# Cross-attention split on GpSimd: one subtraction for both rests, one instruction for each side's two middle parts

## The chip, the cores and the metric

The kernel runs on one core of a Trainium2 chip. The metric is the device time of one launch in microseconds (us). Engines are named as in the profile: PE is TensorE, PEld its weight loads, DVE VectorE, ACT ScalarE, POOL GpSimd, SP SyncE.

## What is computed

One decoder layer in float32 over 32 batch items of 128 rows and 128 channels, in three parts, each followed by a layer norm of the sum with its input: a self-attention with quantised weights, a cross-attention with 16 heads of 8 channels, and a mixture of 8 experts of which each row takes two. The change lies in the cross-attention:

```python
qh = proj(q, Wq, bq); kh = proj(k, Wk, bk); vh = proj(v, Wv, bv)      # 16 heads of 8
scores = jnp.einsum('bhqd,bhkd->bhqk', qh, kh) / jnp.sqrt(hd)
w = jax.nn.softmax(jnp.where(m, -jnp.inf, scores), axis=-1)
out = jnp.einsum('bhqk,bhkd->bhqd', w, vh)
```

## The kernel before, in words

The queries and keys are float32, the matmuls of the scores run in bfloat16. So each value is written as a sum of three bfloat16 parts, high, middle and low, and the parts are laid out in six slots of eight columns for every head (tile `QK`, which the profile calls pair_sq since it shares that memory), so that one matmul over the 48 columns gives the sum of the six products that matter. Queries hold high in slots 0, 2, 4, middle in 1 and 3, low in 5; keys hold high in 3, 4, 5, middle in 0 and 1, low in 2. Behind the slots lie pad columns: the mask, and three parts of minus the row maximum.

The cross-attention is staged by an order written out by hand. A slot handles several batch items at different stages, each engine runs its part of the slot (`b_slot`) in program order, and semaphores join them. Four slots make a tile of four items; the slots are numbered j = 1, 2, 3, 0. Per item, in the order of the work:

- PE projects; DVE adds the biases (line 2190 values, line 2191 `qk_f`, queries and keys together).
- ACT writes the high parts into all their slots (lines 1546 and 1547).
- POOL makes the rest and the other parts (lines 844 to 861). First two subtractions, line 845, one for each side: rest = value minus high. Then a wait for them (`ch.settle()`), the mask column (line 849), four copies of the rest into the middle slots that round it to bfloat16 (line 853), a wait, and two subtractions rest minus middle for the low slots (line 857). The last signals `split_ready`.
- In the next slot PE turns the keys (second half of the 16 transposes of line 1107), waiting for `split_ready`; then the queries.

In the same slot DVE works for other items: the maxima of the scores of an earlier item (line 2179, two halves), the row sums of another (2196 to 2200), a copy of turned keys out of PSUM (2207), and then the chain that splits minus the row maximum into three bfloat16 parts (lines 2215, 2217, 2219, 2221, 2223; five instructions on 16 columns, each waiting for the one before). I call these five the maximum chain. After it a slot's own extra follows: j = 1 picks experts (lines 2025 to 2041), j = 2 the sum and statistics of the second norm (2011, 1861, 1872, 1876), j = 3 places rows (2017, 2047 to 2065).

On POOL, ahead of the split, stand the indirect DMAs that post rows for the experts (line 825, two in a slot), in j = 3 the power of line 802, and in j = 0 the copy and numbering of rows (815, 816). `qk_rest` is only used on POOL.

Of the kernel before, what the change touches and what calls it, by code (L numbers as in the profile page):

```python
# [8 lines left out]
def decoder_layer(nc, x, ctx_1024, mask, wq, wk, wv, wo, Wq, bq, Wk, bk, Wv, bv,  # L9
# [3 lines left out]
    ALU, ACT, AX = mybir.AluOpType, mybir.ActivationFunctionType, mybir.AxisListType  # L13

    B, P, D = x.shape
    H, HD = 16, D // 16
# [31 lines left out]
    with ctx:  # L48
        def sb(name, shape, dt=F32):
            return ctx.enter_context(nc.sbuf_tensor(name, shape, dt))  # L50
# [8 lines left out]
        def after(eng, s, n):  # L59

            eng.wait_ge(s, n + CREDIT)
# [5 lines left out]
        class Chain:  # L67
# [129 lines left out]
        QK = pair_sq[:].rearrange("p a b -> p (a b)").bitcast(BF16)[:, 0:8 * H * HS].rearrange(  # L197
            "p (a b c d) -> p a b c d", a=4, b=2, c=H)
# [64 lines left out]
        qk_f = sb("qk_f", [P, 2, 2, D])  # L263
        qk_rest = sb("qk_rest", [P, 2, D])
# [181 lines left out]
        def batch(t, i):  # L446

            return bass.ds(TB * t + i, 1)
# [35 lines left out]
        def slots(j, side, first, end, by=1):  # L484

            return QK[:, j, side, :, 0:6 * HD].rearrange("p h (s d) -> p h s d", d=HD)[:, :, first:end:by, :]

        def heads(ap):

            return ap.rearrange("p (h d) -> p h d", h=H)  # L490
# [28 lines left out]
        def route_turn(u):  # L519

            return 0 <= u - 3 < T - 1
# [127 lines left out]
        def _(pool):  # L649
            ch = Chain(pool, pool_chain)  # L650
# [148 lines left out]
            def invert_roots(u):  # L799

                after(pool, ve2_ready, u - 1)
                pool.tensor_tensor(rstd2[:], ve2[:], half[:, 0:TB], ALU.pow).then_inc(rstd2_ready, 1)

            def preset_rows():

                after(pool, y_rounded, T)
                ch(pool.memset(staged_h[:, :, :, :, D - 1], X_SCALE))
                pool.memset(staged_h[:, :, :, :, 2 * D - 1], 0.0).then_inc(rows_preset, 1)

            def number_rows(t):  # L810

                if t >= 2:
                    posted_by(pool, t - 2)
                pool.wait_ge(x_lo_ready, t + 1)
                ch(pool.tensor_copy(staged_h[:, t % 2, :, 1, D:2 * D - 1], staged_h[:, t % 2, :, 0, D:2 * D - 1]))
                ch(pool.iota(staged[:, t % 2, :, :, D].bitcast(I32), pattern=[[P, TB], [B * P, 2]], base=NT * t,
                             channel_multiplier=1))
                ch.settle()
                pool.wait_ge(spot_ready, t + 1)
                if t == 0:  # L820
                    pool.wait_ge(padded, 16 * PADS)

            def post_rows(t, i, a):

                pool.indirect_dma_start(xs[:], bass.IndirectOffsetOnAxis(ap=spot_u[:, t % 2, a, i:i + 1], axis=0),  # L825
                                        staged[:, t % 2, i, a, :], None).then_inc(posted[t % 2], 16)

            def b_slot(u, parity, there, j):
                if u == 2 and j == 0:
                    preset_rows()  # L830
                if route_turn(u - 1):
                    if j == 0:
                        number_rows(u - 4)
                    for a in range(2):
                        post_rows(u - 4, j, a)
                k = TB * u + j - 1
                if j == 3 and there(2) and not (isinstance(u, int) and u == T + 1):
                    invert_roots(u)
                l, i = divmod(j - 1, TB)
                if there(-l):  # L840

                    after(pool, split_ready, k)
                    after(pool, high_ready, k + 1)
                    for side in range(2):
                        ch(pool.tensor_tensor(heads(qk_rest[:, side]), heads(qk_f[:, i % 2, side]),  # L845
                                              slots(i, side, 4, 5)[:, :, 0, :], ALU.subtract))
                    ch.settle()

                    pool.tensor_tensor(QK[:, i, 1, :, 6 * HD], ones[:, 0:H],
                                       mask_neg[:, batch(u + l, i)].broadcast_to((P, H)), ALU.mult)  # L850
                    for side, (first, end, by) in enumerate(((1, 4, 2), (0, 2, 1))):
                        for s in range(first, end, by):
                            ch(pool.tensor_scalar(slots(i, side, s, s + 1)[:, :, 0, :],  # L853
                                                  heads(qk_rest[:, side]), 1.0, None, ALU.mult))
                    ch.settle()
                    for side, low in enumerate((5, 2)):
                        last = pool.tensor_tensor(slots(i, side, low, low + 1)[:, :, 0, :], heads(qk_rest[:, side]),
                                                  slots(i, side, 1, 2)[:, :, 0, :], ALU.subtract)
                        if side == 0:
                            ch(last)  # L860
                    last.then_inc(split_ready, 1)
# [4 lines left out]
            prepare_pads()  # L866
            y_rows(T - 2)
            one_slot(b_slot, 0, 1)
            first_scales(T - 2)
            one_slot(b_slot, 0, 2)  # L870
            y_stats(T - 1)
            y_rows(T - 1)
            one_slot(b_slot, 0, 3)
            prepare_frames()
            one_slot(b_slot, 1, 0)
# [1585 lines left out]
```

## Time and profile before

| what | value |
|---|---|
| device time, median of 3 runs | 703.71 us (701.25 to 704.7) |
| device time of the profiled execution | 700.64 us |
| span of the profiled execution | 698.9 us |
| DVE busy | 554.2 us (79%) |
| PE busy | 536.1 us (77%) |
| POOL busy | 476.9 us (68%) |
| ACT busy | 475.1 us (68%) |

The span runs from the first to the last instruction; the rest of the profiled execution's time, 1.74 us, lies around it. The self-attention takes the first 215 us or so, the split of the cross-attention runs from 225 to 480 us, and the experts and the last norm follow. Busy shares are means over these stages, so they do not say which engine sets the pace in one of them; the chain of waits and the timeline of a stretch do.

### The profile page before, as it was taken

What the parts mean: (1) busy time and instruction counts of PE and PEld (TensorE: products, weight loads), DVE (VectorE), ACT (ScalarE), POOL (GpSimd) and SP (SyncE); (2) the same over time, 40 slices, a digit from 0 to 9 for tenths busy, and PEclk for the clock granted to TensorE, in tenths of its full rate; (3) what the DMA queues carried; (4) which work ended last, traced back from release to release, by engine and by line L of the source; (5) the groups of instructions that cost most, each with busy time, mean ns of one, the idle gap of its engine ahead of it and who ended that gap; (6) DMA issues with size and microseconds to landing.
All of it is one profiled execution on the core that took longest, in us unless ns stands there. A gap on an engine that the chain in (4) does not pass through costs nothing.

```text
span 698.9 us, 19343 instructions
## 1 busy us (share of the span) xinstructions
PE 536.1 (77%) x6294; PEld 439.6 (63%) x6308; DVE 554.2 (79%) x1699; ACT 475.1 (68%) x975; POOL 476.9 (68%) x655
## 2 busy tenths in 40 slices
PE   1588889998989856878787878877679999997200
PEld 0277878777879845656565656655458889886200
DVE  4999899999996577687979889798778756687584
ACT  4666689887984565778877887777645555667415
POOL 6367688877886274655678898787557776577653
PEclk9789999999999957899999999999699999999655
DMA  6711222222122524354410100001132333531241
GB/s 173 235 13 20 24 22 25 23 23 25 22 39 64 174 86 151 137 220 152 191 49 23 38 32 30 19 19 36 52 92 83 100 102 102 162 111 48 78 118 60
DMA packets 113106, 55.39 MB, mean 79 GB/s; under 512 B 70624, under 2 KB 103840, under 8 KB 113024
## 3 DMA queue, kind: packets, MB, share of 16 engines
q1 hardware_dynamic: 103984, 25.46, 16.2%
q10 hardware_dynamic: 4496, 19.02, 6.9%
q0 software_dynamic: 4544, 9.84, 4.0%
q8 instruction: 49, 0.80, 0.5%
q14 instruction: 33, 0.27, 0.1%
HBM read 21.25 MB, written 33.05 MB: 78 GB/s over the span
## 4 chain that ended last, share of the span: by engine, by line
PE 34%; DVE 32%; ACT 14%; issue 10%; DMA 4%; POOL 3%; SPq 1%; ACTq 0%; DVEq 0%; POOLq 0%
PE PS L996 11%; DVE m L2179 5%; DVE PS L1916 3%; ACT W_raw L1559 3%; PE PS L1289 2%; PE PS L1306 2%; DVE bn L1861 2%; PE PS L1308 2%; PE PS L1307 2%; DMA W_raw<-in_L_ffn_W_dram 2%; PE PS L1107 2%; DVE W_raw L2292 2%; PE PS L1291 1%; PE PS L1290 1%; PE PS L1117 1%
## 5 line engine op out<-in xcount | busy, mean ns | idle before, releaser
L996 PE MATMUL PS<-prod,ident 128*128 128x144 f32 x1024 | 137.4, 294 | 8.5 <-DVE hctx L1896 8.2
L996 PEld LDWEIGHTS PS<-prod,ident 128*128 128x128 f32 x1024 | 131.6, 196 | 16.3 <-issue 9.1
L765 POOL TENSOR_TENSOR prod<-prod,v 128x2048 f32<-128x2048 f32 x32 | 117.5, 3672 | 31.2 <-ACT prod L1403 31.2
L885 POOL DMA_INDIRECT ys<-W_raw,ids x78 | 76.5, 981 | 29.7 <-issue 18.9
L2179 DVE TENSOR_REDUCE m<-PS 128x8 f32<-128x1024 f32 x64 | 77.8, 1216 | 21.1 <-PE PS L1117 21.1
L2292 DVE SCALAR_TENSOR_TENSOR W_raw<-PS,W_raw 128x512 f16<-128x512 f32 x78 | 52.1, 688 | 36.1 <-ACT W_raw L1624 36.1
L825 POOL DMA_INDIRECT xs<-Y,spot_u x64 | 64.2, 1003 | 23.3 <-issue 13.5
L1916 DVE TENSOR_REDUCE PS<-pair_sq 128x128 f32<-128x1024 f32 x64 | 75.0, 1219 | 0.0
L1117 PE MATMUL PS<-prod 52*128 52x128 bf16 (+1 forms) x1024 | 52.6, 230 | 29.2 <-ACT W_raw L1559 11.6
L1559 ACT ACTIVATE W_raw<-PS 128x1024 f32<-128x1024 f32 x64 | 66.0, 1032 | 5.7 <-PE PS L1117 5.7
L853 POOL TENSOR_SCALAR pair_sq<-qk_rest 128x128 bf16<-128x128 f32 x128 | 68.1, 553 | 0.0
L1107 PE MATMUL PS<-ident,pair_sq 128*128 128x128 bf16 x768 | 59.1, 232 | 9.0 <-ACT prod L1552 8.9
L1107 PEld LDWEIGHTS PS<-ident,pair_sq 128*128 128x128 bf16 x768 | 50.7, 104 | 18.1 <-ACT prod L1552 13.8
L1117 PEld LDWEIGHTS PS<-prod 52*128 52x128 bf16 (+1 forms) x1024 | 31.1, 99 | 48.9 <-ACT W_raw L1559 15.6
L1308 PE MATMUL PS<-W_lo,W_raw 128*128 x312 | 59.7, 221 | 0.0
L1307 PE MATMUL PS<-W_hi,W_raw 128*128 x312 | 59.5, 221 | 0.0
L1306 PE MATMUL PS<-W_hi,W_raw 128*128 x312 | 59.4, 221 | 0.0
L845 POOL TENSOR_TENSOR qk_rest<-qk_f,pair_sq 128x128 f32<-128x128 f32 x64 | 25.9, 426 | 45.5 <-ACT pair_sq L1547 45.2
L1546 ACT CAST pair_sq<-qk_f 128x384 bf16<-128x384 f32 x32 | 16.4, 511 | 54.7 <-DVE qk_f L2191 53.3
L1624 ACT ACTIVATE W_raw<-PS 128x512 f16<-128x512 f32 x78 | 45.4, 595 | 10.3 <-PE PS L1291 8.0
L1640 ACT ACTIVATE W_raw<-PS,w_rows 128x128 f32<-128x128 f32 x78 | 24.3, 364 | 39.1 <-PE PS L1308 36.9
L1200 PE MATMUL PS<-W_raw 128*32 128x128 f32 x1024 | 43.8, 292 | 6.6 <-issue 4.8
(321 smaller groups left out, 1535.9 us busy)
## 6 DMA issues: line engine op xcount, KB each, us to landing
xs<-pad ACTq DMA_DIRECT2D x16, 1152.0 KB, 4.7
Y<-xs SPq DMA_DIRECT2D x39, 144.0 KB
W_raw<-ys SPq DMA_DIRECT2D x16, 256.0 KB, 3.2
W_raw<-in_L_ffn_W_dram SPq DMA_DIRECT2D x1, 2048.0 KB
shuffle<-hctx SPq DMA_DIRECT2D x32, 64.0 KB, 3.0
Y<-shuffle SPq DMA_DIRECT2D x32, 64.0 KB, 1.8
cs<-in_ctx_dram SPq DMA_DIRECT2D x8, 256.0 KB
out_dram<-W_raw SPq DMA_DIRECT2D x8, 256.0 KB, 2.3
```

The costliest lines, as they stand in the source:

```text
L765: pool.tensor_tensor(rows[:, :, 0:D].rearrange("p t (d h) -> p t d h", d=HD), a.broadcast_to((P, H, HD, H)), v.broadcast_to((P, H, HD, H)) ...
L853: ch(pool.tensor_scalar(slots(i, side, s, s + 1)[:, :, 0, :], heads(qk_rest[:, side]), 1.0, None, ALU.mult))
L885: pool.indirect_dma_start(ys[:], bass.IndirectOffsetOnAxis(ap=ids[:, j % KD, s:s + 1].bitcast(U32), axis=0), ou[j % OD][:, s, :], None).th ...
L996: last = pe.matmul(PS[:, 6, 0:TC], ident[:], prod2[:, i % 2, TC * t:TC * (t + 1)], start=(t == 0), stop=(t == H - 1))
L1107: last = pe.transpose(PS[:, bank, g * 64:(g + 1) * 64].bitcast(BF16), QK[:, j, side, HR * g:HR * g + HR, :].rearrange("p h r -> p (h r)"), ...
L1117: last = pe.matmul(PS[:, 2 * a + r, g * P:(g + 1) * P], left[rows, HG // 2 * a + g, :], right[rows, HG // 2 * a + g, :], start=True, stop= ...
L1306: pe.matmul(o, h_hi[j % 2][:, c, tokens], w_hi, start=False, stop=False)
L1307: pe.matmul(o, h_lo[j % 2][:, c, tokens], w_hi, start=False, stop=False)
L1308: last = pe.matmul(o, h_hi[j % 2][:, c, tokens], w_lo, start=False, stop=(c == FC - 1))
L1559: act.activation(half_heads(PT[:, i % 2], a), banks(a).rearrange("p r (g q) -> p r g q", q=P), ACT.Exp, scale=HD ** -0.5).then_inc(p_ready, 1)
L1916: step(dve.tensor_reduce(total, pair_sq[:, i % 2, HD * first_sum:HD * end_sum].rearrange("p (c d) -> p c d", d=HD), AX.X, ALU.add))
L2179: dve.tensor_reduce(half_heads(m2[:], a), banks(a).rearrange("p r (g t) -> p r g t", t=P), AX.X, ALU.max).then_inc(max_done, 1)
```

## The change

The two subtractions of line 845 become one, over both sides (256 elements in each partition instead of 128). The wait between them and the mask column goes. The four copies of line 853 become two subtractions, one for each side: value minus high, written into both middle slots at once (256 elements, both inputs read twice through a broadcast), rounded to bfloat16 on the way out. They read `qk_f` and the high slot, no longer the rest. The wait before the low parts and the two instructions of line 857 stay.

```diff
-                    for side in range(2):
-                        ch(pool.tensor_tensor(heads(qk_rest[:, side]), heads(qk_f[:, i % 2, side]),
-                                              slots(i, side, 4, 5)[:, :, 0, :], ALU.subtract))
-                    ch.settle()
+                    both = QK[:, i].rearrange("p a h r -> p (a h) r")
+                    ch(pool.tensor_tensor(qk_rest[:].rearrange("p a (h d) -> p (a h) d", h=H),
+                                          qk_f[:, i % 2].rearrange("p a (h d) -> p (a h) d", h=H),
+                                          both[:, :, 4 * HD:5 * HD], ALU.subtract))
 
                     pool.tensor_tensor(QK[:, i, 1, :, 6 * HD], ones[:, 0:H],
                                        mask_neg[:, batch(u + l, i)].broadcast_to((P, H)), ALU.mult)
                     for side, (first, end, by) in enumerate(((1, 4, 2), (0, 2, 1))):
-                        for s in range(first, end, by):
-                            ch(pool.tensor_scalar(slots(i, side, s, s + 1)[:, :, 0, :],
-                                                  heads(qk_rest[:, side]), 1.0, None, ALU.mult))
+                        ch(pool.tensor_tensor(slots(i, side, first, end, by),
+                                              heads(qk_f[:, i % 2, side]).unsqueeze(2).broadcast_to((P, H, 2, HD)),
+                                              slots(i, side, 4, 5).broadcast_to((P, H, 2, HD)), ALU.subtract))
                     ch.settle()
```

## Rows read from the trace of the kernel before

**Rows 1.** Chain of waits: start us, length us, engine, tile, line.

```profile
308.64 0.23 DVE pair_sq L2217
...
399.93 0.09 DVE m_neg L2215
...
400.55 0.23 DVE pair_sq L2221
...
400.93 0.69 DVE yq_f L2011
...
469.27 0.24 DVE pair_sq L2217
```

**Rows 2.** DVE's waits from 330 to 476 us: us, times, longest us.

```profile
DVE m L2179 <- PE PS L1117: 8.8, 4, 3.2
```

**Rows 3.** Timeline of DVE in a j = 0 slot: start, us, line, operation, shape.

```profile
417.44 1.23 DVE L2179 TENSOR_REDUCE m<-PS 128x8 f32<-128x1024 f32 x1 [1.67 <-PE PS L1117]
```

**Rows 4.** Timeline of the j = 2 slot that the working follows.

```profile
397.09 0.42 DVE L2191 TENSOR_TENSOR qk_f<-PS,b_qkv 128x256 f32<-128x256 f32 x1
...
398.62 0.81 POOL L845 TENSOR_TENSOR qk_rest<-qk_f,pair_sq 128x128 f32<-128x128 f32 x2 [0.92 <-ACT pair_sq L1547]
...
399.50 0.27 POOL L849 TENSOR_TENSOR pair_sq<-ones,mask_neg 128x16 bf16<-128x16 f32 x1
...
399.68 2.31 POOL L853 TENSOR_SCALAR pair_sq<-qk_rest 128x128 bf16<-128x128 f32 x4
...
402.08 0.81 POOL L857 TENSOR_TENSOR pair_sq<-qk_rest,pair_sq 128x128 bf16<-128x128 f32 x2
...
403.49 1.06 PE L1107 MATMUL PS<-ident,pair_sq 128*128 128x128 bf16 x16
```

**Rows 5.** POOL's groups by shape: count, busy us, mean ns of one, idle before.

```profile
L765 POOL TENSOR_TENSOR prod<-prod,v 128x2048 f32<-128x2048 f32 x32 | 117.5, 3672 | 31.2 <-ACT prod L1403 31.2
...
L853 POOL TENSOR_SCALAR pair_sq<-qk_rest 128x128 bf16<-128x128 f32 x128 | 68.1, 553 | 0.0
...
L845 POOL TENSOR_TENSOR qk_rest<-qk_f,pair_sq 128x128 f32<-128x128 f32 x64 | 25.9, 426 | 45.5 <-ACT pair_sq L1547 45.2
...
L896 POOL TENSOR_TENSOR X<-X,bet 128x512 f32<-128x512 f32 x8 | 10.1, 1261 | 0.0
```

**Rows 6.** Timeline of two stretches where small DVE instructions meet POOL's.

```profile
414.08 0.82 POOL L845 TENSOR_TENSOR qk_rest<-qk_f,pair_sq 128x128 f32<-128x128 f32 x2
...
414.59 0.37 DVE L2217 CAST pair_sq<-m_neg 128x16 bf16<-128x16 f32 x1
...
471.35 0.48 DVE L2056 TENSOR_SCALAR Y<-w_first,o_scale 128x4 f32<-128x4 f32 x1
471.38 0.81 POOL L857 TENSOR_TENSOR pair_sq<-qk_rest,pair_sq 128x128 bf16<-128x128 f32 x2
...
471.75 0.47 DVE L2057 SCALAR_TENSOR_TENSOR Y<-w_first,o_scale,eg 128x4 f32<-128x4 f32 x1
...
472.13 0.61 POOL L815 COPY Y<-Y 128x508 f16<-128x508 f16 x1
472.26 0.50 DVE L2061 TENSOR_TENSOR run<-run,picked 128x8 bf16<-128x8 bf16 x1
```

**Rows 7.** Single lines of DVE: count, duration in ns min/median/max, first and last start.

```profile
L2217 DVE CAST pair_sq<-m_neg x32: 203/223/380, 254.6 to 490.2; 128x16 bf16<-128x16 f32 x32
...
L2221 DVE CAST pair_sq<-m_rest x32: 205/224/244, 255.2 to 490.7; 128x16 bf16<-128x16 f32 x32
...
L2035 DVE CAST topf<-topi x8: 181/318/431, 333.5 to 531.7; 128x32 f32<-128x32 uint32 x8
...
L2056 DVE TENSOR_SCALAR Y<-w_first,o_scale x8: 231/280/481, 347.9 to 535.3; 128x4 f32<-128x4 f32 x8
...
L2057 DVE SCALAR_TENSOR_TENSOR Y<-w_first,o_scale,eg x8: 212/220/468, 348.3 to 535.4; 128x4 f32<-128x4 f32 x8
...
L2061 DVE TENSOR_TENSOR run<-run,picked x8: 154/160/500, 348.8 to 535.7; 128x8 bf16<-128x8 bf16 x8
```

## Prediction, made before the result was known

> **What bounds the kernel now.** I read the profile's busy shares first (the table above), then the chain of waits, then the timeline of single slots. The shares say little here: DVE, PE, POOL and ACT are all between 68 and 79% busy over the whole span. The chain says more. From about 300 to 476 us it runs through DVE in most slots, one instruction behind the other, the maximum chain among them. Its cast of line 2217 stands on the chain 15 times between 308.64 and 469.27 us [rows 1]. These are the batch items 9, 12 to 14, 16 to 18, 20 to 22, 24, 25 and 28 to 30, counted from 0. In the other slots DVE waits for PE: after 330 us four times ahead of line 2179, 8.8 us together, all in j = 0 slots [rows 2], 1.67 us in the one that I show [rows 3].
>
> POOL's split is on no path. In the j = 2 slot shown, the last low part is done at 402.08 + 0.81 = 402.89 us, and PE begins its 16 transposes, of which the second half reads the keys, at 403.49 [rows 4]. So a faster split is waited for by nobody. What it can do is meet other work.
>
> **What the change does to POOL.** I count from the end of `qk_f`, 397.09 + 0.42 = 397.51 us. Before: rests from +1.11, mask at +1.99, four copies from +2.17 to +4.48, low parts from +4.57 to +5.38 [rows 4]. Price of the new instruction, a tensor_tensor on 256 elements, which the trace does not show: 128 elements take 0.426 us, 2,048 take 3.672 [rows 5], a slope of 1.69 ns, so 0.64 us. With 512 elements at 1.261 us [rows 5] as the other end the slope is 2.17 ns and the price 0.70. The cheap end comes from the mask, 16 elements in 0.27 us [rows 4]: a slope of 1.39 ns from there to 128, so 0.60. I take 0.64, since line 765, the only one of them with a broadcast of three levels, lies on that line. Neighbours overlap by 0.04 us (two of 0.426 take 0.81 [rows 4, 5]), and from mask to the next instruction it is 0.18 [rows 4].
>
> After: rest +1.11 to +1.75; mask at +1.71; first middle pair +1.89 to +2.53; second +2.49 to +3.13; the wait that stays, 0.08; low parts +3.21 to +4.02. POOL saves about 1.1 us for each of 32 items, some 35 us of busy time, and the wait that went (0.08) is in it. The posts of the next slot (line 825) start so much earlier when their addresses are there; on the chain nobody waits for them in this stage. Worth of all this on the path: zero, and its cover is the 0.6 us between 402.89 and 403.49, which only grows.
>
> **What it does to DVE.** The maximum chain starts at 399.93, +2.42, and the next instruction (line 2011) at 400.93, +3.42 [rows 1]. Before, all of it lay beside the four copies of line 853. After, it lies beside the second middle pair and the low parts, which are tensor_tensor. That is not the same to DVE, as the trace shows.
>
> Beside tensor_tensor: at 414.59 the cast of line 2217 takes 0.37 us in place of 0.20, and ends 0.06 behind the second L845 (414.08 + 0.82 = 414.90) [rows 6, 7]. At 471.35 line 2056 takes 0.48 in place of 0.23, at 471.75 line 2057 takes 0.47 in place of 0.21, each ending just behind one of the two L857 that run back to back from 471.38 to 472.19; and line 2061 takes 0.50 in place of 0.15, ending behind the copy of line 815 at 472.74 [rows 6, 7]. So a small DVE instruction on SBUF that meets one of these on POOL waits until it ends, and the two alternate: each POOL instruction costs one DVE instruction its length.
>
> Beside the copies of line 853 nothing of this happens: line 2221, at 400.55 in the midst of them [rows 1, 4], never takes over 0.244 us in 32 executions, against 0.205 at best; the median loss is 0.02 [rows 7].
>
> The Trainium skill (SBUF — State Buffer, section "Who interferes with whom") says that VectorE and GpSimd share a pair of ports, that whichever instruction issues first holds it to its end, and that the order of issue decides and not the kind of operation. The tensor_tensor rows agree with it; line 853, a tensor_scalar that reads SBUF as well, does not. By the rule the copies would have held DVE up just as long, and less POOL time could only help; that is the third rival below.
>
> So the chain after: line 2215 starts at +2.42 and waits for the first middle pair until about +2.56, 0.05 later than before. Line 2217 waits for the second pair, +3.13, and ends near +3.19. Line 2219 then starts behind the first low part (+3.21) and waits for its end, +3.64; line 2221 waits for the second, +4.02, and ends near +4.07; line 2223 starts at +4.10 and the next instruction 0.12 behind it, +4.22. Before it was +3.42. **The price is 0.8 us for an item whose maximum chain is on the path.** If line 2219 slips in front of the first low part, one wait falls away and it is some 0.3 less. The second pair ends at 1.21 + 3 times the price of an instruction: at 0.70 us an item costs 1.0, at 0.60 it costs 0.7, and 0.4 if line 2219 slips in as well.
>
> What comes back: line 2035 met the low parts in the j = 1 slots (median 0.318 against 0.181 [rows 7]), and POOL will be done by then: 0.14 an item, with line 2038 about 0.2. Lines 2056, 2057 and 2061 lost 0.25, 0.26 and 0.35 in two j = 3 slots, at item 30 [rows 6] and alike at item 14, near 348 us (their first starts in [rows 7]); that is 0.85 for each, less about 0.1 for the copy of line 815, which then runs earlier and meets them.
>
> **The sum.** j = 2, the 6 items 9, 13, 17, 21, 25, 29: 6 x 0.8 = 4.8. j = 1, the 5 items 12, 16, 20, 24, 28: 5 x (0.8 - 0.2) = 3.0. j = 3, items 18 and 22: 2 x 0.8 = 1.6; items 14 and 30: 0.8 - 0.75, nothing. Together 9.4 us. All other items have slack: in the j = 0 slots the 1.67 us [rows 3] takes up 0.8, and item 26, which is not on the chain, ends in the longest of the four waits, 3.2 us [rows 2]. Against the profiled execution: 700.64 (span 698.9 and 1.74 around it) + 9.4 = 710.0. That execution is 3.1 us, 0.4%, under the median of the three runs; from the median, 703.71, the same sum gives **713.1**, and I name 713.
>
> Ends: all items at 0.4 give 2.4 + 1.0 + 0.8 less 0.7 for items 14 and 30, 3.5, or 707.2. All at 1.0 give 6.0 + 4.0 + 2.0 + 0.5, with item 26 coming onto the path 1.0 more, 13.5, or 717.2. From the profiled execution the low end is 704.1.
>
> **The rivals.** First, the new subtractions are dearer: 256 elements as two of 128, 0.81 us. Then the second pair ends at 1.21 + 3 x 0.81 = +3.64, the next instruction starts at +4.73, and an item costs 1.3: 6 x 1.3 + 5 x 1.1 + 2 x 1.3 + 2 x 0.55 + 1.3 = 18.3, or 722. Against it: from 128 to 512 elements the time grows 3.0 times, to 2,048 only 8.6 times [rows 5].
>
> Second, the small DVE instructions are not held by the new forms: both their inputs read bfloat16 and float32 through broadcasts, and no row shows that form beside them. Then only what comes back is left, 5 x 0.2 + 2 x 0.75 = 2.5: 701.2, within the bound. For it: of the forms that hold DVE, lines 845, 857 and 815, none has three levels. Against it: their length and kind, two inputs, are the same.
>
> Third, on the other side: **DVE gets there first and POOL is the one that waits.** In the slot shown the four copies take 2.31 us in place of four at about 0.5, since line 2011 runs beside them [rows 4]; so POOL does wait for DVE. If every POOL instruction that reads SBUF holds DVE alike or not at all, as line 853 does, then what stands beside DVE falls from 4.27 us (+1.11 to +5.38) to 2.91 an item, and DVE gets back all that it lost: 5 x 0.2 + 2 x 0.85 = 2.7 us, and the 0.02 that three of the five instructions lose on each of the 15 items, 0.9. Together 3.6 us, 700.1, just beyond the bound. The rule of the Trainium skill named above (SBUF — State Buffer) leads here. It decides from the point where a maximum chain passes three tensor_tensor instructions without a wait. Against it are the rows of lines 2056, 2057 and 2061.
>
> **How the numbers follow.** My forecast, 0.4 to 1.0 us for an item, 72%. The dearer instruction 8%. Not held 15%. POOL waits 5%. The forecast and the first rival are slower by over 0.5%, about what a measurement of this kernel tells from no change (3.5 us, so above 707.2); the second rival is within 0.5%, the third is faster. So faster 0.05, same 0.15, slower 0.80. The range runs from 705, about the low end against the profiled execution, to 719, the high end of the forecast and some of the dearer instruction.
>
> **What would show it.** In the changed profile: POOL's new tensor_tensor on 256 elements at 0.60 to 0.70 us; its split done at about +4.0 behind `qk_f`; lines 2217 and 2221 with medians near 0.4 us where they have 0.22 now, line 2219 likewise; the period of the j = 1 and j = 2 slots longer by 0.6 and 0.8 us; the median of line 2035 at 0.18; nobody waiting for the low parts, as now. It is wrong if those medians stay at 0.2, or if the j = 0 slots show no wait any more, which would mean that their slack was too small for 0.8 us.

## The result, and the profile after

The changed kernel takes 714.77 us, the median of 4 runs (712.93 to 716.0), beside 702.48 us (699.95 to 704.7) for the kernel before: ratio 1.017, 95% interval 1.0137 to 1.0202, so 12.3 us slower. 713 was predicted. The profiled execution of the changed kernel has a span of 714.3 us.

POOL is less busy and DVE more. Page of the changed kernel, busy time (before, in the table above: DVE 554.2, POOL 476.9 us):

```profile
PE 541.4 (76%) x6308; PEld 443.9 (62%) x6308; DVE 576.8 (81%) x1699; ACT 475.7 (67%) x975; POOL 442.5 (62%) x559
```

POOL saves 34.4 us, and DVE is 22.6 us longer busy with the same instructions. The groups of POOL by shape, changed kernel, which answer to [rows 5] (busy us, mean ns of one, idle before):

```profile
L852 POOL TENSOR_TENSOR pair_sq<-qk_f,pair_sq 128x256 bf16<-128x256 f32 x64 | 39.7, 642 | 0.0
...
L845 POOL TENSOR_TENSOR qk_rest<-qk_f,pair_sq 128x256 f32<-128x256 f32 x32 | 21.5, 671 | 77.5 <-ACT pair_sq L1547 77.3
```

The new instruction takes 0.64 us for the middle parts and 0.67 for the rests; 0.64 was the price in the sum. DVE's side, single lines of the changed kernel (count, ns min/median/max, first and last start), which answer to [rows 7]:

```profile
L2217 DVE CAST pair_sq<-m_neg x32: 202/595/717, 255.9 to 505.4; 128x16 bf16<-128x16 f32 x32
...
L2219 DVE TENSOR_TENSOR m_rest<-m_neg,pair_sq x32: 186/451/1347, 256.2 to 505.6; 128x16 f32<-128x16 f32 x32
...
L2221 DVE CAST pair_sq<-m_rest x32: 206/372/591, 256.7 to 505.9; 128x16 bf16<-128x16 f32 x32
...
L2035 DVE CAST topf<-topi x8: 181/181/182, 339.0 to 546.9; 128x32 f32<-128x32 uint32 x8
...
L2061 DVE TENSOR_TENSOR run<-run,picked x8: 152/154/158, 355.4 to 550.8; 128x8 bf16<-128x8 bf16 x8
```

The middle of the maximum chain has doubled: line 2217 had a median of 223 ns, line 2221 one of 224. Lines 2035 and 2061 have lost their collisions and now always take their shortest time. The same j = 2 slot as in [rows 4], timeline of POOL and of DVE, changed kernel:

```profile
407.74 0.67 POOL L845 TENSOR_TENSOR qk_rest<-qk_f,pair_sq 128x256 f32<-128x256 f32 x1 [2.65 <-ACT pair_sq L1547]
408.37 0.26 POOL L849 TENSOR_TENSOR pair_sq<-ones,mask_neg 128x16 bf16<-128x16 f32 x1
408.54 1.24 POOL L852 TENSOR_TENSOR pair_sq<-qk_f,pair_sq 128x256 bf16<-128x256 f32 x2
409.86 0.81 POOL L857 TENSOR_TENSOR pair_sq<-qk_rest,pair_sq 128x128 bf16<-128x128 f32 x2
```

```profile
408.97 0.24 DVE L2215 TENSOR_SCALAR m_neg<-m 128x16 f32<-128x16 f32 x1
409.24 0.60 DVE L2217 CAST pair_sq<-m_neg 128x16 bf16<-128x16 f32 x1
409.87 0.45 DVE L2219 TENSOR_TENSOR m_rest<-m_neg,pair_sq 128x16 f32<-128x16 f32 x1
410.36 0.37 DVE L2221 CAST pair_sq<-m_rest 128x16 bf16<-128x16 f32 x1
410.76 0.23 DVE L2223 TENSOR_TENSOR pair_sq<-m_rest,pair_sq 128x16 bf16<-128x16 f32 x1
```

Read the ends. The two middle parts run to 409.78, and line 2217 ends at 409.84. The low parts end near 410.28 and at 410.67, and lines 2219 and 2221 end at 410.32 and 410.73. Three links of the chain, each some 0.05 us behind one POOL instruction. From the start of line 2215 to the start of line 2223, which is what I call the time of the chain, it is now 1.79 us; it was 0.95. All over the trace, 79 of the 88 links (lines 2217, 2219, 2221) that run beside these subtractions end 0.03 to 0.10 us behind the end of one of them.

Slot by slot (from the end of one `qk_f` to the end of the next, worked out from the timelines of both kernels):

| slots | before, us | after, us | difference, sum | in the prediction |
|---|---|---|---|---|
| j = 2, items 9, 13, 17, 21, 25, 29 | 7.27 to 7.28, item 29 7.89 | 8.11 to 8.12, item 29 8.75 | +5.05 | +4.8 |
| j = 1, items 12, 16, 20, 24, 28 | 7.33 to 7.35, item 16 7.63 | 8.01 to 8.02 | +3.07 | +3.0 |
| j = 3, items 18 and 22 | 7.25 | 8.06, 8.11 | +1.67 | +1.6 |
| j = 3, items 14 and 30 | 8.01, 8.02 | 8.05, 8.23 | +0.25 | 0 |
| j = 3, item 26 | 7.25 | 8.43 | +1.18 | absorbed |
| j = 0, items 11, 15, 19, 23, 27 | 8.72, 8.66, 8.05, 8.04, 9.53 | 10.27, 7.92, 8.92, 7.92, 8.68 | +0.71 | 0 |

Together 11.9 us. The spans differ by 15.4; 2.4 of the rest lie ahead of item 9 and 1.1 behind item 31; of the 2.4, 1.5 lie ahead of the first `qk_f`, where no changed instruction has run yet, and 0.9 in items 0 to 8. The medians, which are the measurement, differ by 12.3.

### The profile page after: what moved, and what is told of

Its sections match the earlier page's. It is cut to its first block, busy times and chain, and to the rows that moved or that the text cites. A ratio compares the mean times of both kernels' runs of the same rounds, so it can differ in the third digit from the quotient of the medians.

```text
span 714.3 us, 19261 instructions
## 1 busy us (share of the span) xinstructions
PE 541.4 (76%) x6308; PEld 443.9 (62%) x6308; DVE 576.8 (81%) x1699; ACT 475.7 (67%) x975; POOL 442.5 (62%) x559
## 4 chain that ended last, share of the span: by engine, by line
PE 35%; DVE 31%; ACT 11%; issue 10%; POOL 6%; DMA 4%; SPq 1%; DVEq 0%; ACTq 0%; POOLq 0%
PE PS L996 11%; DVE m L2179 5%; DVE PS L1916 3%; POOL ys L885 2%; ACT W_raw L1559 2%; PE PS L1107 2%; PE PS L1289 2%; PE PS L1306 2%; PE PS L1308 2%; PE PS L1307 2%; DMA W_raw<-in_L_ffn_W_dram 2%; DVE prod L2207 2%; PE PS L1291 1%; PE PS L1290 1%; DVE pair_sq L2217 1%
## 5 line engine op out<-in xcount | busy, mean ns | idle before, releaser
L845 POOL TENSOR_TENSOR qk_rest<-qk_f,pair_sq 128x256 f32<-128x256 f32 x32 | 21.5, 671 | 77.5 <-ACT pair_sq L1547 77.3
L1107 PE MATMUL PS<-ident,pair_sq 128*128 128x128 bf16 x768 | 61.0, 236 | 9.9 <-ACT prod L1552 9.9
L1107 PEld LDWEIGHTS PS<-ident,pair_sq 128*128 128x128 bf16 x768 | 52.8, 107 | 19.3 <-ACT prod L1552 15.1
L1307 PE MATMUL PS<-W_hi,W_raw 128*128 x312 | 58.7, 219 | 0.0
L1306 PE MATMUL PS<-W_hi,W_raw 128*128 x312 | 58.6, 218 | 0.0
L1289 PE MATMUL PS<-W_raw,W_hi 128*128 128x256 f16 x156 | 42.8, 275 | 1.3 <-issue 0.8
```

The source lines that it names most:

```text
L1107: last = pe.transpose(PS[:, bank, g * 64:(g + 1) * 64].bitcast(BF16), QK[:, j, side, HR * g:HR * g + HR, :].rearrange("p h r -> p (h r)"), ...
L1306: pe.matmul(o, h_hi[j % 2][:, c, tokens], w_hi, start=False, stop=False)
L1307: pe.matmul(o, h_lo[j % 2][:, c, tokens], w_hi, start=False, stop=False)
```

## The experiments

The theory of the prediction was that two-input POOL instructions hold DVE's small SBUF instructions and the copies of line 853 do not. The rival was the rule that I had set aside: every POOL instruction that reads the SBUF holds them, whatever its kind. In these kernels line numbers shift by a few; the links of the chain are named by their operands.

**One half of the change, the rests.** The two rests in one instruction; the wait and the four copies as before:

```diff
-                    for side in range(2):
-                        ch(pool.tensor_tensor(heads(qk_rest[:, side]), ...
+                    ch(pool.tensor_tensor(<rests of both sides>, <qk_f>, <high slots>, ALU.subtract))
                     ch.settle()
```

> Only the two rests are made by one instruction; the wait behind them and the four copies of the rest into the middle slots stay. Theory (tensor_tensor on POOL holds DVE's small SBUF instructions, tensor_scalar does not): the maximum chain still lies beside the copies, so its step from line 2215 to line 2223 stays at 0.95 us in the steady slots and the time is that of the kernel before, 700 to 705 us. Rival (an earlier split slows the kernel in some other way, through PE or the posts): a part of the loss, in the share of POOL time saved, 0.15 of 1.1 us, so about 2 us, 704 to 706.

Measured 708.58 us (707.62 to 709.07) beside 700.65, ratio 1.0101 (1.0072 to 1.013). Both theories said less. In a j = 2 slot the copies start some 0.14 us earlier against the chain, and the slot goes from 7.28 to 7.54 us. The chain takes 1.07 us, and the add of the second norm, behind it, begins together with the last copy and takes 0.15 us longer. Single lines of this kernel, the add and the copies (before, the add took 0.69 us [rows 1]):

```profile
L2012 DVE TENSOR_TENSOR yq_f<-att,X x8: 681/834/839, 312.9 to 522.0; 128x512 f32<-128x512 f32 x8
...
L854 POOL TENSOR_SCALAR pair_sq<-qk_rest x128: 517/524/550, 229.5 to 485.1; 128x128 bf16<-128x128 f32 x128
```

In j = 3 slots line 2057 of this kernel stands behind the copy of line 815 (median 0.692 us, shortest 0.232). So the copies of line 853 do hold DVE, and the kernel before lost so little to them since its chain stood well against them. The slots of j = 1, 2 and 3 from item 9 on are some 5 us longer in all. Not all of the loss is theirs: in the profiled execution 3.3 us lie ahead of the first `qk_f`, where nothing altered has run yet.

**The other half, the middle parts.** The two rests as before, without the wait; the middle parts as in the change:

```diff
-                        for s in range(first, end, by):
-                            ch(pool.tensor_scalar(slots(i, side, s, s + 1)..., heads(qk_rest[:, side]), 1.0, None, ALU.mult))
+                        ch(pool.tensor_tensor(slots(i, side, first, end, by), <qk_f twice>, <high twice>, ALU.subtract))
```

> Only the middle parts are changed: one tensor_tensor for each side, straight from the values; the rests stay two instructions. Theory: the chain waits as in the changed kernel, and 0.15 us longer, since the middle pairs end that much later: the step from line 2215 to line 2223 is 1.95 us in place of 1.79, and with 16 such items on the path the time is 714 to 719 us. Rival (what counts is how early the split is done): a little better than the changed kernel, 712 to 714.

Measured 716.15 us (715.3 to 717.57), ratio 1.0206 (1.0177 to 1.0236). The first cast of the chain has a median of 0.596 us, as in the changed kernel, and the chain takes 1.93 us, as the theory had it. This half alone costs as much as the whole change; the costs of the two halves do not add up to it (1.0 and 2.1% against 1.7%).

**The kind of the middle instruction, 256 elements.** Rest merged, with a wait behind it, and one multiplication by one for each side's two middle parts:

```diff
+                        ch(pool.tensor_scalar(slots(i, side, first, end, by), <rest twice>, 1.0, None, ALU.mult))
```

> One instruction for the rests, and one tensor_scalar for each side's two middle parts, from the rest through a broadcast; so POOL has as few instructions as in the changed kernel, but the middle parts have one input from memory. Theory: the tensor_scalar does not hold DVE whatever its length; the chain stays at 0.95 us, and the low parts come earlier, so that line 2035 and lines 2056 to 2061 meet them less: 698 to 703 us. Rival (every POOL instruction of 256 elements holds DVE): chain near 1.8 us and 712 to 718.

Measured 715.46 us (713.77 to 719.88), ratio 1.0213 (1.0164 to 1.0262): my theory fell, the rival held in its time. Timeline of POOL, then of DVE, in a j = 3 slot of this kernel:

```profile
416.74 1.68 POOL L853 TENSOR_SCALAR pair_sq<-qk_rest 128x256 bf16<-128x256 f32 x2
418.50 0.84 POOL L858 TENSOR_TENSOR pair_sq<-qk_rest,pair_sq 128x128 bf16<-128x128 f32 x2
```

```profile
417.25 0.41 DVE L2218 CAST pair_sq<-m_neg 128x16 bf16<-128x16 f32 x1
417.69 0.31 DVE L2220 TENSOR_TENSOR m_rest<-m_neg,pair_sq 128x16 f32<-128x16 f32 x1
418.04 0.44 DVE L2222 CAST pair_sq<-m_rest 128x16 bf16<-128x16 f32 x1
```

The first multiplication ends at 417.60, the second at 418.42. Links 1 and 3 end 0.06 us behind them, at 417.66 and 418.48. But the link between ends at 418.00, in the midst of the second one, 0.43 us after its start, and half of 0.85 is 0.42. In all, 48 of 84 links beside these multiplications end 0.03 to 0.10 us behind one, and 29 others 0.43 to 0.46 us after one has begun. So a multiplication by one holds DVE too, but lets an instruction through half-way. The chain takes 1.45 us, and its last link, beside the low parts, 0.50 instead of 0.23.

That is what hid the effect in the kernel before. There 42 of 80 links end just behind a copy, and 30 others 0.32 to 0.37 us after the start of one, when half of it (0.26) has gone; the other 8 had begun before the copy. A held piece is then 0.25 us long, and a link with what lies before the next takes 0.22 to 0.24 by itself: no more time to lose.

**Number and place as before, kind changed.** Four subtractions of 128 elements in place of the four copies:

```diff
-                            ch(pool.tensor_scalar(slots(i, side, s, s + 1)..., heads(qk_rest[:, side]), 1.0, None, ALU.mult))
+                            ch(pool.tensor_tensor(slots(i, side, s, s + 1)..., heads(qk_f[:, i % 2, side]), <high>, ALU.subtract))
```

> The kernel before with each of the four copies replaced by a subtraction value minus high of the same 128 elements; count, length and order of the POOL instructions stay, only the kind changes. Theory: each holds one instruction of the maximum chain for up to 0.4 us; the step from line 2215 to line 2223 becomes 1.4 to 1.6 us, line 2223 waits as well, and an item loses 0.7 to 0.9 us: 711 to 717 us. Rival (the length of 256 elements or the broadcast of three levels is what holds DVE): chain 0.95 to 1.1 us and 700 to 705.

Measured 717.08 us (714.53 to 719.38), ratio 1.023 (1.0187 to 1.0273). The theory held, at the upper end of its range. Single lines of this kernel, the chain's first cast and its last link:

```profile
L2217 DVE CAST pair_sq<-m_neg x32: 203/381/388, 255.7 to 505.1; 128x16 bf16<-128x16 f32 x32
...
L2223 DVE TENSOR_TENSOR pair_sq<-m_rest,pair_sq x32: 231/496/505, 256.8 to 505.8; 128x16 bf16<-128x16 f32 x32
```

The links go at the pace of the subtractions, one about every 0.39 us, and the chain takes 1.50. That looks better than the 1.79 of the changed kernel, but here line 2223 waits too. In the j = 2 slots it is 2.00 us from the start of line 2215 to the end of line 2223, beside 2.02 in the changed kernel, and the slots take 8.08 us beside 8.11. Four subtractions of 128 elements cost as much as two of 256.

**The same as a plain cast.** The four copies as casts without arithmetic:

```diff
-                            ch(pool.tensor_scalar(slots(i, side, s, s + 1)..., heads(qk_rest[:, side]), 1.0, None, ALU.mult))
+                            ch(pool.tensor_copy(slots(i, side, s, s + 1)[:, :, 0, :], heads(qk_rest[:, side])))
```

> The kernel before with its four middle parts written by a plain cast of the rest (one input, no arithmetic) in place of the multiplication by one; number, size and place of the instructions stay. Theory (every GpSimd instruction that reads the SBUF holds VectorE's small SBUF instructions while it runs, and the multiplication by one does so only in part of its time, as the runs so far suggest): a cast is like the 0.61 us cast of line 815, in whose time line 2056 took 0.33 us instead of 0.23; each link of the maximum chain then starts at the end of a cast, the chain takes 1.3 to 1.8 us against 0.95, and the time is 709 to 717. Rival (only instructions with two inputs hold): chain 0.95 to 1.0, time 699 to 704.

Measured 705.11 us (703.13 to 707.4) beside 702.68, ratio 1.0041 (1.002 to 1.0061): between the two. Single lines of this kernel, the chain's first cast and its last link, POOL's casts, and the long add of j = 3:

```profile
L2216 DVE CAST pair_sq<-m_neg x32: 203/206/216, 254.4 to 490.9; 128x16 bf16<-128x16 f32 x32
...
L2222 DVE TENSOR_TENSOR pair_sq<-m_rest,pair_sq x32: 229/500/507, 255.2 to 491.6; 128x16 bf16<-128x16 f32 x32
...
L853 POOL CAST pair_sq<-qk_rest x128: 287/297/313, 226.0 to 478.6; 128x128 bf16<-128x128 f32 x128
...
L2046 DVE SCALAR_TENSOR_TENSOR Y<-X,Y x8: 678/918/923, 347.2 to 536.5; 128x508 f16<-128x508 f32 x8
```

The cast is done in 0.30 us instead of 0.52, and one begins every 0.24. The chain's links end some 0.06 us behind a cast each, but at a pace of 0.24 us, which is their own: nothing lost (chain 0.91 us). What is lost comes after: the low parts now start earlier, and their two subtractions meet the last link (0.50 instead of 0.23) and line 2046 (0.92 instead of 0.68).

**Another offset.** The kernel before with a memset of 64 elements in each partition on POOL ahead of the four copies:

```diff
+                    pool.memset(idle_tile[:], 0.0)
                     for side, (first, end, by) in enumerate(((1, 4, 2), (0, 2, 1))):
```

> The kernel before with one small memset on GpSimd (64 elements a partition of a tile that nobody reads) ahead of its four middle copies: all copies and low parts start 0.1 to 0.3 us later, all else stays. Theory (the chain ran free of the copies in the kernel before only because its steps happened to fall between them): with another offset the links meet the copies' ends, the chain takes 1.05 to 1.3 us and the time is 703 to 710. Rival (copies never hold anything): chain 0.95 and 699 to 703.

Measured 704.22 us (700.73 to 705.78), ratio 1.0023 (1.0001 to 1.0044). The chain takes 1.05 us, the j = 2 slots 7.38. This offset against the copies is worth 0.1 us a slot, about what the chain itself lost in the half with the rests.

**The chain out of reach.** The changed kernel, and the kernel before, with the chain's two float32 tiles in PSUM, so that no link has more than one operand to read in the SBUF; to share the bank DVE waits for its own copy and PE for the chain:

```diff
-        m_neg = sb("m_neg", [P, H])
-        m_rest = sb("m_rest", [P, 1, H])
+        m_neg = PS[:, 5, 0:H]
+        m_rest = PS[:, 5, H:2 * H]
...
+                    after(dve, kT_ready, min(k, B))
```

> The changed kernel with the negated maximum and its rest kept in PSUM, so that no link of the maximum chain has more than one operand to read in the SBUF. It adds a wait of VectorE on its own copy ahead of the chain (the bank is shared with the transposed keys) and a wait of TensorE on the chain, which ends long before. Theory (the chain is slow only since its links wait for GpSimd's instructions at the SBUF): four of its five links escape, the chain comes back from 1.79 us to 1.0 to 1.3, the slots of steps 2 from 8.1 us to 7.3 to 7.6, and the time is 702 to 708. Rival (the loss is from something else that the change moves: an earlier split, other semaphores): 712 to 717, whatever the chain takes.

> The kernel before with the same placement of the negated maximum and its rest in PSUM, and the same two waits, as the changed kernel had in e6. It prices that placement alone, so that e6 less this run is what the change costs where the chain is out of GpSimd's reach. Theory (the chain is most of the change's cost; what is left are the collisions of other lines): the added wait costs 0.1 us in some 24 items, the chain 1.0 to 1.1 us, time 703 to 706, and e6 is above it by 2 to 5 us where the changed kernel is above the kernel before by 12. Rival (the chain is not where the change costs): e6 is above this run by 8 us or more, so this run is at 700 or below.

Measured, changed kernel so altered: 707.93 us (705.66 to 710.45), ratio to before 1.0072 (1.0043 to 1.0101). Kernel before so altered: 705.49 us (703.84 to 711.2), ratio 1.0073 (1.0046 to 1.0099). The placement costs 3.5 us in itself; on top of it the change costs 2.4 us by the medians and nothing by the ratios, where it costs 12.3 with the chain in the SBUF. The two intervals together leave some 3 us either way, an estimate from their widths. The chain takes 0.96 us in both, in each of 32 executions. The chain's first cast in the altered changed kernel, and POOL's middle parts there, single lines:

```profile
L2221 DVE CAST pair_sq<-PS x32: 228/230/233, 255.4 to 494.9; 128x16 bf16<-128x16 f32 x32
...
L852 POOL TENSOR_TENSOR pair_sq<-qk_f,pair_sq x64: 633/642/653, 226.8 to 482.4; 128x256 bf16<-128x256 f32 x64
```

Within 5 ns in 32 executions, 29 of them beside the same subtractions that stretched it to 0.6 us. The j = 2 slots take 7.47 us in both altered kernels. The j = 3 slots 18, 22 and 26 stay 0.24 to 0.31 us longer (7.65 to 7.71 against 7.41), since the low parts meet the long add, line 2050 there (median 0.93 us).

**Another place.** The changed kernel with its two middle instructions held until the chain is done:

```diff
+                    if there(-((j - 3) // TB)):
+                        after(pool, m_ready, k - 1)
                     for side, (first, end, by) in enumerate(((1, 4, 2), (0, 2, 1))):
```

> The changed kernel with a wait of GpSimd on the maximum chain ahead of its two middle instructions: the same four instructions, in another place. Theory (place is what costs: the same instructions cost nothing beside work that reads PSUM): chain 0.95 to 1.05 us, steps 2 back to 7.2 to 7.4 us; the middle and low parts come 1 us later, where they meet lines 2035, 2038 and 2056 to 2061 of steps 1 and 3 instead; 701 to 708. Rival (the split's end has become late for TensorE, as my cover of 0.6 us says it might): the slots of steps 2 wait for the transposes, 709 to 716.

Measured 705.34 us (703.34 to 709.61), ratio 1.0045 (1.0021 to 1.0069). The chain is back at 0.90 us and the j = 2 slots at 7.32; 9.4 of 12.3 us are won back with the same four instructions. PE does not wait for the later split. What remains is in j = 3: items 18, 22 and 26 take 8.15 to 8.17 us. POOL in one of these slots, then DVE, timelines of this kernel:

```profile
408.33 1.05 POOL L802 TENSOR_TENSOR rstd<-ve,half 128x4 f32<-128x4 f32 x1
409.36 0.66 POOL L845 TENSOR_TENSOR qk_rest<-qk_f,pair_sq 128x256 f32<-128x256 f32 x1
409.99 0.26 POOL L849 TENSOR_TENSOR pair_sq<-ones,mask_neg 128x16 bf16<-128x16 f32 x1
411.11 1.64 POOL L854 TENSOR_TENSOR pair_sq<-qk_f,pair_sq 128x256 bf16<-128x256 f32 x2 [0.87 <-DVE pair_sq L2225]
```

```profile
409.51 0.55 DVE L2217 TENSOR_SCALAR m_neg<-m 128x16 f32<-128x16 f32 x1
...
410.98 0.68 DVE L2049 SCALAR_TENSOR_TENSOR Y<-X,Y 128x508 f16<-128x508 f32 x1
...
411.69 0.49 DVE L2054 TENSOR_SCALAR eg<-eg 128x4 f32<-128x4 f32 x1
```

Since POOL finished the split of the slot before later, its posts and the power of line 802 came later, and so the rest: it ends at 410.02, and the chain's first link, 0.16 us at best, at 410.06. The middle parts then meet line 2054 (0.49 instead of 0.15). There is a second reading in these rows: the first middle part takes about 1.0 us instead of 0.64, since line 2049 had begun before it and ran to 411.66. Whoever has begun goes on; the other waits, be it POOL or DVE.

**Casts, and the low parts late.** The kernel before with the four casts, and the wait for the chain ahead of the two low parts:

```diff
                     ch.settle()
+                    if there(-((j - 3) // TB)):
+                        after(pool, m_ready, k - 1)
                     for side, low in enumerate((5, 2)):
```

> The kernel before with the four middle parts as plain casts (as in e5) and a wait of GpSimd on the maximum chain ahead of its two low parts, whose two-input subtractions met the chain's last link and line 2046 in e5. Theory (casts hold nothing, two-input subtractions hold to their end, and place decides what they meet): chain 0.9 us, its last link 0.23 instead of 0.50, line 2047 0.68 instead of 0.92; the slots of steps 2 take 7.15 to 7.3 us; the low parts now meet lines 2052 to 2061 of steps 3 for 0.2 to 0.5 us; time 698 to 703, so at or below the kernel before. Rival (the low parts cost as much wherever they stand, or the split becomes late for TensorE): 705 to 710.

Measured 702.93 us (700.47 to 706.03) beside 702.02, ratio 1.0005 (0.9984 to 1.0026). The chain takes 0.91 us with its last link at 0.23, the j = 1 slots fall to 7.12 to 7.14 us and the j = 2 slots to 7.23. All j = 3 slots stand between 7.7 and 8.0, where items 18, 22 and 26 were at 7.25 and items 14 and 30 at 8.0: the copy of line 815 now meets line 2057 in each of them (median 0.69 us, shortest 0.23), which was more than expected.

**The changed kernel's count, with casts.** One instruction for the rests, one cast for each side's two middle parts, low parts late:

```diff
+                        ch(pool.tensor_copy(slots(i, side, first, end, by), <rest twice>))
```

> The number of GpSimd instructions of the changed kernel (one for the rests, one for each side's two middle parts), with the middle parts as one plain cast of the rest to two places instead of a subtraction, and the low parts after the chain as in e10. Theory (the form costs, not the merging): the 256-element casts take 0.45 to 0.6 us, the chain 0.9 to 1.0 us, time 698 to 704. Rival (every GpSimd instruction of 256 elements holds, as the multiplication of 256 elements did in e3): chain 1.4 us or more, 711 to 717.

Measured 704.74 us (702.0 to 708.19), ratio 1.0036 (1.0019 to 1.0053), just above the range of the theory. Single lines of this kernel, the chain's first cast and POOL's:

```profile
L2219 DVE CAST pair_sq<-m_neg x32: 202/285/341, 256.2 to 492.5; 128x16 bf16<-128x16 f32 x32
...
L853 POOL CAST pair_sq<-qk_rest x64: 392/402/420, 227.9 to 479.8; 128x256 bf16<-128x256 f32 x64
```

A cast of 256 elements takes 0.40 us and holds as well: 34 of the 38 links beside these casts end 0.03 to 0.10 us behind one. There are only two, and both are nearly over when the chain begins, so the chain takes 0.98 us.

**And the copy late.** The kernel with casts and late low parts, and the wait of line 815's copy for the row numbers moved ahead of it:

```diff
                 pool.wait_ge(x_lo_ready, t + 1)
+                pool.wait_ge(spot_ready, t + 1)
                 ch(pool.tensor_copy(staged_h...
                 ...
-                pool.wait_ge(spot_ready, t + 1)
```

> The kernel of e10 with the copy of line 815 held back until the row numbers are done (its wait for them moved ahead of it), since in e10 line 2057 stood 0.69 instead of 0.23 us behind that copy. Theory (place decides): line 2057 back to 0.23 us, the copy beside the next reduction from PSUM, the slots of steps 3 fall from 7.7 to 7.2 to 7.4 us, time 697 to 702, at or below the kernel before. Rival (steps 0, which wait for TensorE's scores, take up what the others give): the steps 3 fall and the steps 0 grow by as much, time 701 to 705.

Measured 700.95 us (696.51 to 702.89) beside 701.71, ratio 0.9987 (0.997 to 1.0004): the best of all kernels here, though not told from the kernel before. Line 2057 of this kernel, single line:

```profile
L2057 DVE TENSOR_SCALAR Y<-w_first,o_scale x8: 230/231/232, 347.7 to 534.3; 128x4 f32<-128x4 f32 x8
```

All five j = 3 slots take 7.25 us. That the whole moves by less than these slots has one reason in the profiled execution: item 23, a j = 0 slot, takes 9.54 us where it took 8.04, in a stretch with TensorE at its lower clock (last section). The rival's trade, j = 3 against j = 0, is not what it is: items 15 and 19 are at 8.05 us.

## Why the prediction was right, and where it was not

- **The price of the new instruction: right.** 0.64 us forecast, 0.642 measured, 0.671 for the rests.
- **The chain's new timetable: right.** Forecast ends behind `qk_f`: line 2217 +3.19, line 2219 +3.64, line 2221 near +4.07. In the j = 2 slot shown (`qk_f` ends at 406.63) they are +3.21, +3.69 and +4.10. The low parts end at +4.04 (forecast +4.02). 0.84 us a slot instead of 0.8. The chain starts at +2.34 and not at +2.42, since [rows 1] has only the piece of line 2215 that the copy before it leaves; no end hangs on it. Line 2217 waits out a whole middle part, so its median is 0.595 us where "near 0.4" was named. That the loss is the chain's, and the hold at the SBUF its cause, the two runs with the chain in PSUM show.
- **What comes back: right.** Line 2035 is at 0.181 us, and four of the five j = 1 slots lose 0.66 to 0.68 us where the chain alone loses 0.84. Items 14 and 30 cost +0.04 and +0.21 against nothing.
- **POOL off the path: right.** It saved 34 us of busy time and nobody got any of it. Even where the split of a j = 2 slot ended at +6.03 instead of +4.04, in the run with another place, PE did not wait for it.
- **Slack in the j = 0 slots: right, but little of it is left.** DVE's wait for PE ahead of line 2179 fell from 8.8 us [rows 2] to 6.5, still four times. Three of the four are in slots that a stretch of TensorE at its lower clock reaches into (last section). In item 23, which has none in either kernel, 1.67 us [rows 3] became 0.46, and in item 15 there is no wait any more; neither slot is longer for it. Timeline of the changed kernel:

```profile
428.14 1.22 DVE L2179 TENSOR_REDUCE m<-PS 128x8 f32<-128x1024 f32 x1 [0.46 <-PE PS L1117]
```

- **Item 26 at nothing: wrong.** The 3.2 us that were to take it up belong to one execution, in which PE's 16 transposes ran at the lower clock (1.61 us instead of 1.06 [rows 4]). In the changed kernel the maximum chain in item 26's slot is on the chain of waits. Chain of waits around item 26, kernel before, then the changed kernel:

```profile
441.80 1.61 PE PS L1107 x16
```

```profile
449.52 0.60 DVE pair_sq L2217
```

In the eight traces here that have no such stretch in item 27, that item takes 7.92 to 7.94 us whether item 26 took 7.36 or 8.33: it takes up nothing. So item 26 belongs in the sum with the price of items 18 and 22.
- **The size: 12.3 us by the medians and 11.9 in the slots of the profiled pair, against 9.4.** The forecast terms measured 10.0. Of the other 1.9, 1.2 are item 26, and 0.7 are the j = 0 slots, by the clock. That 713 lies within 2 us of 714.77 is in part luck: the sum started from the median of three runs, 703.71, which with the fourth is 702.48.
- **The step that failed: "beside the copies of line 853 nothing of this happens".** They hold too. What looked like no hold was a hold of about 0.25 us at a time, as long as a link takes anyway, and a chain that stood well against it: an earlier split by 0.14 us, with all that it then met, cost some 5 us of slots in the half with the rests. So the choice against the rule was made for a wrong reason. The Trainium skill (SBUF — State Buffer, section "Who interferes with whom") says that the order of issue decides and not the kind of operation. On the kind the runs agree: subtraction, multiplication by one and cast all hold. On "to its end" they agree for subtractions and casts; the multiplication let a link through half-way, at 418.00 in one that ran from 417.57 to 418.42. The third rival, which followed that rule to 700.1 us, counted only how long POOL works beside DVE. What costs is by how much each held piece is longer than the link that waits: some 0.01 us for copies and casts of 128 elements (the chain takes 0.95 and 0.91 us beside them, 0.90 beside nothing), 0.15 for subtractions of 128 (1.50 us over four steps), 0.4 for a subtraction of 256 (0.60 us for line 2217 instead of 0.20). Over the whole chain the two kinds of subtraction come to the same. The sum came out since it priced the new instructions by rows of their own kind.
- The first rival (0.81 us an instruction) fell with 0.642, the second (not held) with line 2217.

## What to carry to other kernels

Before you merge small GpSimd instructions beside a chain of short VectorE instructions on the SBUF, compare the length of one GpSimd instruction with the pace of the chain, since each link waits out one of them. Casts that follow each other every 0.24 us cost a chain with links every 0.23 us almost nothing. Four subtractions of 0.43 us cost it as much as two of 0.64, since more links wait. So keeping the instructions short helps only as far as they come down to the pace of the chain. If a stretch shows no collision, look whether that is the instruction's kind or only its offset; the ends of the short instructions, held against the ends of the long ones, tell. Then move the long ones to where VectorE reads PSUM, and follow every instruction queued behind them.

## What the runs showed of the hardware that was not expected

The multiplication by one is the slow way to cast on GpSimd: 0.52 us for 128 elements and 0.85 for 256, where a cast takes 0.30 and 0.40 and a subtraction with two inputs 0.43 and 0.64.

The granted clock of TensorE explains the j = 0 slots. Busy time in stretches around item 11, changed kernel, then the kernel before (window, length, busy of PE, PEld, DVE, ACT, POOL, granted clock, DMA share, GB/s):

```profile
321.00:323.00 2.00, 1.25 (x12) 0.75 (x12) 1.56 (x3) 2.00 (x7) 0.00 (x0) 1.00 0.98 394
...
324.00:326.00 2.00, 2.00 (x23) 1.66 (x21) 1.93 (x5) 1.12 (x2) 1.74 (x4) 0.50 0.03 12
```

```profile
317.00:319.00 2.00, 1.35 (x20) 0.97 (x20) 1.23 (x1) 2.00 (x6) 1.37 (x4) 1.00 0.90 348
...
321.00:323.00 2.00, 2.00 (x39) 1.43 (x37) 2.00 (x4) 1.88 (x2) 1.86 (x5) 1.00 0.03 12
```

PE had been about as busy in both just before. Then the clock fell to 0.50, its lower level of 1.2 GHz, in the changed kernel and not in the other; the 16 transposes of line 1107 there took 1.91 us instead of 1.06, and the j = 0 slot of item 11 10.27 us instead of 8.72. Such stretches of 3 to 7 us lie around items 11, 19, 26 to 27 and 30 in the changed kernel's execution, and around 15, 27 and 29 to 30 in the other's, so items 15 and 27 went the other way. In the traces of all fourteen kernels here the j = 0 slots from item 15 on take 7.92 to 8.05 us without such a stretch and 8.43 to 9.57 with one; item 11 takes 8.71 or 8.72 without one and 10.20 to 10.27 in the three that have it throughout. Whether a slower DVE brings more of them, single executions do not tell; that stays open.
